# A two-layer recurrence with attention: gates i and g, the mixed values and h's part packed in 32 columns, and the softmax's division moved behind the mixing

## What is computed

```python
def _lstm_cell(x, h, c, Wi, Wh, bi, bh):
    g = x @ Wi.T + bi + h @ Wh.T + bh
    i, f, gg, o = jnp.split(g, 4, axis=-1)
    c2 = sigmoid(f) * c + sigmoid(i) * tanh(gg)
    h2 = sigmoid(o) * tanh(c2)
    return (h2, c2)

def step(carry, x_t):
    h0, c0, h1, c1, a = carry
    xin = jnp.concatenate([x_t, a], axis=-1)
    h0, c0 = _lstm_cell(xin, h0, c0, Wi0, Wh0, bi0, bh0)
    h1, c1 = _lstm_cell(h0, h1, c1, Wi1, Wh1, bi1, bh1)
    q = h1 @ Wq.T
    attn = softmax(einsum('bh,bsh->bs', q, context), axis=-1)
    mixed = einsum('bs,bsh->bh', attn, context)
    a2 = tanh(concatenate([mixed, h1], axis=-1) @ Wo.T + bo)
    return ((h0, c0, h1, c1, a2), a2)
```

## Time and profile before

| | |
|---|---|
| three runs | 8253.83, 8262.45, 8263.24 us (median 8262.45) |
| the profiled execution | 8255.78 us; its span 8254.0 us |
| busy in the span | PE 6793.0 us (82%), PE weight loads 5788.2 (70%), VectorE (DVE) 4208.6 (51%), ScalarE (ACT) 3382.8 (41%), GpSimd (POOL) 313.9 (4%) |
| the recurrence | from about 89 to 7296 us of the span, 1024 steps of 7.03 us |
| what follows it | 7296 to 8254 us |

### The profile page before, as it was taken

How to read it: one execution, slowest core, us unless ns; L and a number is a source line. 1 busy time by engine, 2 the same in 40 slices (tenths; PEclk the granted TensorE clock), 3 DMA queues, 4 the chain that set the end, 5 groups by cost and what they waited for, 6 DMA issues and landing times. The chain is left out here.

```text
span 8254.0 us, 814880 instructions
## 1 busy us (share of the span) xinstructions
PE 6793.0 (82%) x380441; PEld 5788.2 (70%) x380449; DVE 4208.6 (51%) x21164; ACT 3382.8 (41%) x17073; POOL 313.9 (4%) x334
## 2 busy tenths in 40 slices
PE   7888888888888888888888888888888888868769
PEld 5777777777777777777777777777777777746546
DVE  5554555555455545455445555555555544466822
ACT  4444444444444444444444444444444444452422
POOL 0000000000000000000000000000000000002532
PEclk8999999999999999999999999999999999989889
DMA  2000000000000000000000000000000000000143
GB/s 87 5 0 0 5 0 0 0 0 5 0 0 0 5 0 0 0 2 4 0 0 0 5 0 0 0 5 0 0 0 0 5 0 0 0 14 11 70 164 109
DMA packets 94641, 102.08 MB, mean 12 GB/s; under 512 B 46570, under 2 KB 81904, under 8 KB 93424
## 3 DMA queue, kind: packets, MB, share of 16 engines
q1 hardware_dynamic: 89200, 88.73, 3.5%
q0 software_dynamic: 5376, 12.63, 0.4%
HBM read 79.75 MB, written 23.67 MB: 13 GB/s over the span
## 5 line engine op out<-in xcount | busy, mean ns | idle before, releaser
L353 PE MATMUL scan_sums<-rec_wh,scan_hT 128*4 128x64 f32 x131008 | 2392.3, 219 | 3.3 <-issue 3.3
L476 DVE STREAM_TRANSPOSE scan_sums<-scan_sums 128x64 f32<-128x64 f32 x6144 | 1552.2, 265 | 1126.1 <-PE scan_sums L353 1111.4
L353 PEld LDWEIGHTS scan_sums<-rec_wh,scan_hT 128*4 128x4 f32 x131008 | 1989.6, 89 | 3.8 <-issue 3.8
L353 PE MATMUL scan_sums<-rec_wa,scan_aT 128*4 128x64 f32 (+1 forms) x65536 | 1103.8, 219 | 381.7 <-ACT scan_aT L435 381.7
L353 PEld LDWEIGHTS scan_sums<-rec_wa,scan_aT 128*4 128x4 f32 (+1 forms) x65536 | 914.9, 88 | 570.6 <-ACT scan_aT L435 570.6
L353 PE MATMUL scan_sums<-rec_wx,scan_xT 128*4 128x64 f32 (+1 forms) x65536 | 1292.1, 219 | 7.2 <-issue 6.3
L353 PE MATMUL scan_sums<-rec_wi,scan_hT 128*4 128x64 f32 (+1 forms) x65536 | 1102.6, 219 | 145.0 <-issue 3.7
L353 PEld LDWEIGHTS scan_sums<-rec_wi,scan_hT 128*4 128x4 f32 (+1 forms) x65536 | 913.6, 88 | 333.7 <-DVE scan_hT L567 329.9
L353 PEld LDWEIGHTS scan_sums<-rec_wx,scan_xT 128*4 128x4 f32 (+1 forms) x65536 | 1024.2, 89 | 7.9 <-issue 6.9
L419 ACT ACTIVATE scan_tanh_f<-scan_sums 128x8 f32<-128x8 f32 x2048 | 364.0, 178 | 1216.4 <-DVE scan_sums L476 1216.4
L414 ACT ACTIVATE scan_sums<-rec_bias 128x192 f32<-128x192 f32 x2050 | 686.7, 335 | 301.2 <-PE scan_sums L393 5.7
(11 more groups left out here) (262 smaller groups left out, 6104.6 us busy)
## 6 DMA issues: line engine op xcount, KB each, us to landing
experts_bias<-in_b SPq DMA_DIRECT2D x40, 640.0 KB, 4.3
moe_w<-in_w SPq DMA_DIRECT2D x16, 1024.0 KB, 12.5
slots_x<-route_blank SPq DMA_DIRECT2D x40, 129.0 KB, 2.3
experts_x<-slots_x SPq DMA_DIRECT2D x40, 129.0 KB
w_xres<-in_x_steps SPq DMA_DIRECT2D x8, 512.0 KB, 12.8
w_xres<-in_x SPq DMA_DIRECT2D x4, 1024.0 KB, 12.1
x_rows<-w_xres SPq DMA_DIRECT2D x4, 1024.0 KB
a_rows<-scan_stage SPq DMA_DIRECT2D x224, 16.0 KB, 1.5
```

Source lines behind the costliest of these rows:

```text
L353: last = nc.tensor.matmul(sums[layer][BANK[g]][32 * j:32 * j + ROWS[g], 0:64], state[:, k, FIRST[g]:FIRST[g] + ROWS[g]], weight[:, k, j, 6 ...
L476: nc.vector.transpose(turned[l][g], sums[l][g][:, 0:64]).then_inc(gates_turned[l][g], 1)
```

## The change

1. **i and g in 32 columns.** Each gate's 64 columns are cut in halves. The state's buffer has 3B zeros ahead of its B columns and 3B behind it; a window of 16 columns (`WIDE`) puts the state in rows 0 to 3 (i, first half), 4 to 7 (i, second half), 8 to 11 and 12 to 15 (g). All write the same 32 columns of the bank. i and g have 16 matmuls of 32 columns each where they had 8 of 64. `turn` and the tanh read 32 columns instead of 64.
2. **h's part of a and the mixed values** the same, with windows of 8 columns and two halves (`halves_product`): 16 matmuls of 32 columns each where there were 8 of 64. They have separate places in PSUM.
3. **Unnormalised mixing.** The exponentials are transposed and multiplied with the values as they are; the total comes from 8 matmuls with a column of ones (`spread_total`). Then a = mixed x (1 / total) + h's part, in one VectorE instruction, and a transpose of 32 columns from SBUF.
4. **h1 is written twice**: first a copy of both sequences' columns side by side for the scores (`h_twice`), then the state.
5. **PE's loop** holds one step; there is one x buffer instead of two, with a semaphore `x_used` that ScalarE waits for before it refills it.
6. **Around it**: the slots are blanked during the recurrence; in `route` the SP queue issues x's rows and w1, and w2 is issued in `scatter`; ScalarE instead of VectorE copies the normalised rows there. PE waits for w1 at the start of `experts` and for w2 ahead of a down product.

```diff
                 def product(layer, state, weight, gates=(GATE_F, GATE_I, GATE_G, GATE_O), done=None):
...
                     for g in gates:
+                        packed = g in (GATE_I, GATE_G)
+                        for half in range(2 if packed else 1):
+                            for k in range(2):
+                                for j in range(4):
+                                    if packed:
+                                        out = sums[layer][IG][32 * j:32 * j + WIDE, 0:32]
+                                        rows = window(state, k, 2 * (g == GATE_G) + half, 4)
+                                        columns = weight[:, k, j, 64 * g + 32 * half:64 * g + 32 * half + 32]
+                                    else:
+                                        out = sums[layer][BANK[g]][32 * j:32 * j + B, 0:64]
+                                        rows = state[:, k, 3 * B:4 * B]
+                                        columns = weight[:, k, j, 64 * g:64 * g + 64]
...
+                    pe.wait_ge(twice_ready, n)
+                    score_product().then_inc(scores_done, 1)
                     pe.wait_ge(h_ready[1], n + 1)
-                    head_product(scores, state_of(hT[1]), w["kp"], True, True).then_inc(scores_done, 1)
-                    head_product(a_sum, state_of(hT[1]), w["woh"], True, False)
+                    halves_product(a_sum, lambda k, half: window(hT[1], k, half, 2), w["woh"]).then_inc(h_summed, 1)
                     if not last:
                         product(0, hT[0], w["wh0"], (GATE_O,))
                         pe.wait_ge(x_ready, n + 1)
-                        product(0, xT[(s + 1) % 2], w["wx"], (GATE_F, GATE_I, GATE_G))
-                    pe.wait_ge(probs_ready, n)
-                    head_product(a_sum, pT[:], w["vp"], False, True).then_inc(a_summed, 1)
+                        product(0, xT, w["wx"], (GATE_F, GATE_I))
+                    pe.wait_ge(h_kept, n)
+                    pe.wait_ge(exps_turned, n)
+                    for k in range(2):
+                        for j in range(4):
+                            last_total = nc.tensor.matmul(spread_total[32 * j:32 * j + 2 * B, :], expsT[:, 32 * k + B:32 * k + 3 * B], ones[:],
+                                                          start=k == 0, stop=k == 1, skip_group_check=True)
+                    last_total.then_inc(total_spread, 1)
+                    halves_product(mixed, lambda k, half: expsT[:, 32 * k + 2 * B * (1 - half):32 * k + 2 * B * (2 - half)], w["vp"]).then_inc(a_terms, 1)
                     if not last:
-                        product(0, xT[(s + 1) % 2], w["wx"], (GATE_O,))
+                        product(0, xT, w["wx"], (GATE_G, GATE_O)).then_inc(x_used, 1)
...
-                    nc.scalar.activation(exps[:], scores[:, 0:S + 1], ACT.Exp, bias=neg_max[:],
-                                         accum_out=total).then_inc(exps_done, 1)
+                    nc.scalar.activation(exps[:], scores[:, 0:S], ACT.Exp, bias=neg_max[:]).then_inc(exps_done, 1)
...
                         make_a(t + s + 1)
-                        take_x(t + U, s)
+                        act.wait_ge(x_used, t + s + 2)
+                        take_x(t + s + 2)
...
+                        if l == 1:
+                            copies = lambda t: t[:, None, :].broadcast_to([P, 2, 2 * B])
+                            nc.vector.scalar_tensor_tensor(h_twice[:].rearrange("p (c b) k -> p c (b k)", c=2), copies(tanh_o[l][:]), 1.0,
+                                                           copies(tanh_c[l]), ALU.add, ALU.mult).then_inc(twice_ready, 1)
...
+                    dve.wait_ge(h_summed, n)
+                    nc.vector.tensor_scalar(from_h[:], a_sum[:, 0:32], 1.0, None, ALU.mult).then_inc(h_kept, 1)
                     dve.wait_ge(exps_done, n)
-                    nc.vector.reciprocal(inv[:], total).then_inc(inv_done, 1)
-
-                    nc.vector.transpose(expsT[:].rearrange("p k s -> p (k s)"), exps[:, 0:S]).then_inc(p_turned, 1)
-                    dve.wait_ge(inv_done, n)
-                    nc.vector.transpose(invT[:], inv[:].broadcast_to([P, 32])).then_inc(p_turned, 1)
-                    dve.wait_ge(p_turned, 2 * n)
-                    nc.vector.tensor_tensor(pT[:], expsT[:, :, 0:B], invT[:, None, 0:B].broadcast_to([P, 2, B]),
-                                            ALU.mult).then_inc(probs_ready, 1)
-                    dve.wait_ge(a_summed, n)
-                    nc.vector.transpose(a_sumT, a_sum[:, 0:64]).then_inc(a_turned, 1)
+                    nc.vector.transpose(expsT[:, B:B + S], exps[:]).then_inc(exps_turned, 1)
+
+                    dve.wait_ge(total_spread, n)
+                    nc.vector.reciprocal(inv[:], spread_total).then_inc(a_terms, 1)
+                    dve.wait_ge(a_terms, 2 * n)
+                    nc.vector.scalar_tensor_tensor(a_natural[:], mixed, inv[:], from_h[:], ALU.mult, ALU.add).then_inc(a_scaled, 1)
+                    dve.wait_ge(a_scaled, n)
+                    nc.vector.transpose(a_sumT, a_natural[:]).then_inc(a_turned, 1)
...
-                with sp.Fori(0, SLOT_TILES) as j:
-                    sp.dma_start(slots_x[bass.ds(j * P, P), :], blank[:]).then_inc(filled, 16)
+                for b in range(B):
+                    sp.dma_start(x_rows[b].rearrange("(g p) d -> p g d", p=P), xres[:, :, b, :]).then_inc(w["x_kept"], 16)
                 for e in range(E):
                     sp.dma_start(w["w1"][:, e, :, :], ins["w1"][e].rearrange("(c p) n -> p c n", p=P)).then_inc(w["loaded"], 16)
-                for e in range(E):
-                    sp.dma_start(w["w2"][:, e, :, :], ins["w2"][e].rearrange("(f p) n -> p f n", p=P)).then_inc(w["loaded"], 16)
```

More of the change, by code:

```diff
@@ L350, in product @@
                     for g in gates:
+                        packed = g in (GATE_I, GATE_G)
[10 more added lines that the diff above has]
+                                        columns = weight[:, k, j, 64 * g:64 * g + 64]
+                                    last = nc.tensor.matmul(out, rows, columns, start=False,
+                                                            stop=done is not None and g != GATE_I and k == 1 and (half == 1 or not packed),
+                                                            skip_group_check=True)
@@ L351, in product, with halves_product @@
+                def halves_product(out, rows_of, weight):
+                    for half in range(2):
                         for k in range(2):
                             for j in range(4):
-                                last = nc.tensor.matmul(sums[layer][BANK[g]][32 * j:32 * j + ROWS[g], 0:64],
-                                                        state[:, k, FIRST[g]:FIRST[g] + ROWS[g]],
-                                                        weight[:, k, j, 64 * g:64 * g + 64], start=False,
-                                                        stop=done is not None and g != GATE_I and k == 1, skip_group_check=True)
@@ L357, in product @@
-                        if done is not None and g != GATE_I:
-                            last.then_inc(done[BANK[g]], 1)
-                def head_product(bank, state, weight, start, stop):
-                    for k in range(2):
-                        for j in range(4):
-                            last = nc.tensor.matmul(bank[32 * j:32 * j + B, 0:64], state[:, k, :], weight[:, k, j, :],
-                                                    start=start and k == 0, stop=stop and k == 1, skip_group_check=True)
-                    return last
@@ L1654, in bias_rows @@
         rows = np.zeros((4, 32, GATES, 64), bias.dtype)
[L1655 to L1656 removed]
+        blocks = gate_blocks(bias)
+        for g in (0, 3):
+            rows[:, 0:B, g, :] = blocks[g][:, None, :]
+        for at in range(4):
+            g, half = 1 + at // 2, at % 2
+            rows[:, B * at:B * at + B, g, 0:32] = blocks[g][:, None, 32 * half:32 * half + 32]
         return rows.reshape(P, GATES, 64)
```

157 lines of the change are left out of this document (91 added, 66 removed).

## The result

The changed kernel takes **8497.7 us** (median of 4 runs, 8494.2 to 8499.8) where the kernel before, run beside it, takes 8261.2 (8253.8 to 8263.2): ratio 1.0285, 95% interval 1.0272 to 1.0298. It is slower by 2.9%; 8102 us was predicted. The profiled execution's own time is 8499.8 us.

What follows compares the result with a forecast made beforehand. The recurrence's dependency chain, 7.03 us a step with no engine full, was taken as the bound. Terms summed to -0.137 us a step, -140 us over 1024, and -14 behind it: 8255.8 to 8102 us, range 7965 to 8240.

Steps and rivals of the forecast that it cites:

- layers, with h1 twice: Both layers' gates: later last quad but shorter transpose, -0.046 us a step; writing h1 twice, +0.01.
- exponentials to PE: Head up to the mixing: read-out, reciprocal, second transpose and its product gone, 1.08 us becomes 0.63, -0.45 a step.
- first total to the scaling: Head, totals and mixing on PE: 0.47 us becomes 0.60, +0.13 us a step.
- the scaling with its hop: Head, new VectorE instruction with a per-partition factor: 245 ns plus a hop of 0.04, +0.285 us a step.
- last transpose, to a's tanh: End of the head: transpose of 32 columns, SBUF to PSUM, 0.20 us instead of 0.266, -0.066 a step.
- the tail: Behind the recurrence: without blanks and with w2 behind, the scatter follows VectorE, -14 us (ends -20 and +5).
- the narrow quad at 29.5 ns: PE's 32-column matmuls: four across the strips cost 27 ns streaming plus 3 overhead, from quads measured at 64 and 128 columns.
- the bounds 28 and 56: Ends for a 32-column quad on PE: 28 ns by pure proportion, 56 ns with no gain from fewer columns.
- narrow quads are not cheap: Slower rival, PE's narrow products: decides from 33.6 ns a quad; 8500 us at 40 ns (8%), 9624 us at 56 (4%).
- The hop to PE (0.05): Head, from the exponentials' transpose on VectorE to PE's first matmul: 0.05 us, part of the 0.63 up to the mixing.
- the second rival: VectorE takes the gain back: dearer transposes and factor's instruction, 0.15 us a step, 8256 us; chance 10%.
- PE's loop of one step: nothing: End of PE's step: the loop's branch lies in the wait for a and costs nothing.

Runs made afterwards that it cites:

- run 3: Changed kernel with stationaries of 4 columns in place of 16 for gates i and g; 8488.5 us, ratio 1.0285 to the kernel before.
- run 5: Changed kernel with the matmuls of gates i and g cut to 16 of their 32 columns, same number of matmuls; 8492.9 us, ratio 1.0292.
- Run 2: Changed kernel with the head as in the kernel before, gates i and g still packed; 8468.6 us, ratio 1.0260.
- run 1: Changed kernel with gates i and g as in the kernel before, the new head kept; 8320.7 us, ratio 1.0083.
- Run 4: Changed kernel with PE's two waits ahead of the totals in the other order; 8403.8 us, ratio 1.0181.
- run 6: Changed kernel with f's second half, four wide matmuls, put behind the first 12 narrow matmuls of i; 8456.4 us, ratio 1.0247.
- run 8: Changed kernel with gates i and g as before, the totals' two waits swapped, gate g of x's product ahead of the mixing; 8279.6 us, ratio 1.0034.
- run 9: As run 8, but with gate g of x's product behind the mixing, as in the changed kernel; 8240.9 us, ratio 0.9981.
- run 7: Run 2's kernel with gate g of x's product ahead of the mixing; 8407.6 us, ratio 1.0190.

## Why the prediction was wrong

Each term against the median of the steps' records (us a step):
```
term                                   predicted   measured
layers, with h1 twice                    -0.036      +0.165
scores to exponentials                    0          +0.005
exponentials to PE                       -0.45       -0.341
first total to the scaling               +0.13       +0.162
the scaling with its hop                 +0.285      +0.286
last transpose, to a's tanh              -0.066      -0.038
sum                                      -0.137      +0.239
```
The difference of 0.376 us, x 1024, is 385 us; with the start's 9 and the tail's 1 it makes 8497 of the 8500.

**The step that failed is the narrow quad at 29.5 ns**, "since two measured widths lie on one line". The line is right as far as it goes: the first narrow quads take 29 ns. But a long series of narrow quads is slower than the line: behind the tenth quad they come at 33.3 ns, one matmul per 16.7 ns, which no quad of 56 ns can show. I take this for the pace at which PE is handed matmuls. Runs 3 and 5 show that neither the load's width nor the columns matter to it. The average in a gate set is 35.5 ns, 15 quads x 6 ns = 0.09 us in each layer; by so much more than forecast i and g's transpose is late. I had taken the bounds 28 and 56 from the shape of the matmul, and the growth of PE's records (736 to 1152 a step) only as an argument of the rival. That rival, "narrow quads are not cheap", is what happened: its point of decision, 33.6 ns, was passed, and its price for 35.5 would be 8102 + 6 x 38 = 8330 us (the seven of the mixing, which averaged 31 ns, make it some 30 us less). Run 2 puts 0.15 us a step on the gates, where I had forecast a gain of 0.046, and in run 1, without them, the layers are back at 2.11 us.

The Trainium skill's rule that I had set against it (TensorEngine Tiling (Array Packing), Instruction Overhead: up to some 60 columns a matmul costs the same) gave the right sign for another reason: 64 columns took 56 ns a quad, 32 took 29 and 16 took 25, so the array does gain down to about 32. That the gain stops there fits the floor of about 25 ns from start to start in the Trainium skill's TensorE: Matmul & The Clock Gate (section "Wait — 56ns, not 53.3ns?"), if it is read for each strip: the four strips' records start 7 ns apart.

**The hop to PE (0.05)** was copied from a matmul with one wait. The change put two on one, and the one written second, which here comes last, got an instruction of its own: 0.09 us a step, 95 us. I said of the change's new waits only that they are early; the early one was indeed early, and its presence cost. Run 4 shows it.

The transposes gained less than by width: 232 ns for 128x32 from PSUM (taken: 218), 227 for the last (200), 245 for the exponentials' (227, the same shape, then behind another instruction). That is 0.07 us a step together, the second rival's direction and half its size. Groups of the changed kernel, count | busy us, mean ns | idle before:
```profile
L515 DVE STREAM_TRANSPOSE scan_sums<-scan_sums 128x32 f32<-128x32 f32 x2048 | 474.4, 232 | 572.8 <-PE scan_sums L372 565.1
L627 DVE STREAM_TRANSPOSE scan_a_sum<-scan_a_natural 128x32 f32<-128x32 f32 x1024 | 232.2, 227 | 35.3
```

**Right** were the scaling at 245 ns (251), PE still waiting for h0 and h1, x's one buffer, and the tail: -12.8 us for -14. The room ahead of h0 shrank, though: from the start of PE's last matmul record to that of wi1 x h0's first it is 0.243 us where it was 0.357. The weight loads' waits for h0, before and after (us in total, times, longest):
```profile
PEld scan_sums L353 <- DVE scan_hT L567: 328.9, 1019, 0.4
```
```profile
PEld scan_sums L372 <- DVE scan_hT L612: 205.9, 986, 0.2
```
The scatter starts 1.6 us after VectorE's last router instruction and is not slowed by w2 (45.6 us to the first slot, 45.5 before). The tile views of the changed kernel (executions, length ns, first and last start us):
```profile
L1426 DVE CAST moe_expert<-route_expert_f x1: 184/184/184, 8109.1 to 8109.1; 128x40 int32<-128x40 f32 x1
```
```profile
L1441 POOL DMA_INDIRECT slots_x<-moe_rows,moe_slot x32: 956/960/1307, 8110.7 to 8150.2; - x32
L1482 SPq DMA_DIRECT2D experts_x<-slots_x x40: 332/333/372, 8156.3 to 8458.7; - x40
```
"PE's loop of one step: nothing" holds here (0.54 us lie behind x's last matmul) and would not have with the gates alone.

The start's 9 us were not in the sum. Waits from 78 to 100 us in the changed kernel:
```profile
PEld scan_sums L372 <- issue: 6.2, 6, 4.6
PE scan_sums L372 <- issue: 5.4, 4, 4.5
```
PE stands on "issue" for up to 4.6 us at a time in the first step. All kernels with packed gates start 5 to 10 us late (first a's tanh at 82.9 to 88.0 us against 78.2), those with the old gates, which send the blanks too, 0 to 2 us. It fits PE's longer code being fetched for the first time, but I tested only that it goes with the gates.

## What to carry to other kernels

Before splitting matmuls into more and smaller ones, count instructions of the engine as well as its array time: when many follow a wait on the critical path, look in the trace for the pace of a long run of short ones, and if none is there, take the number of instructions as a cost of its own. Order matters too: run 6 won back 0.039 us a step with the same matmuls, by putting wide ones where the slow quads come. And when a change adds a second wait to an instruction on the path, put the one that comes last directly on it; in this program that was the wait written first.

## What the runs showed of the hardware

- Issued round the four strips after a wait, about 20 of the program's matmuls ran at a pace that follows their columns (56, 29 or 25 ns a quad), then three quads of 42 to 75 ns, then one matmul per 16.7 ns, with stationaries of 4 or 16 columns and with 16 or 32 moving columns alike. Without an idle stretch ahead (run 8) the quick part was missing: totals and mixing took 0.400 us in place of 0.364 (run 9). What makes the dip, and whether the 16.7 ns is the pace of handing over, is open.
- Two waits ahead of one matmul: 0.146 us from VectorE's end to PE's first matmul; 0.054 with the two in the other order (run 4). The extra semaphore instruction is 0.051 us long in the trace.
- A loop's end on PE (a branch of 0.208 us, and a register instruction that ends 0.30 us after the branch's start) was covered with 0.54 us from the start of the step's last matmul to the next step's first, and cost 0.056 us with 0.35 (runs 2 and 7).
- A quad of one-column matmuls took 25 to 28 ns, of 16 columns 25, of 32 columns 29, of 64 columns 56.
